# Token mixer: who empties the PSUM banks, when, and how the angles are read

## What is computed

```python
dt = jnp.exp(log_dt)                                   # 128 heads
dt_Lambda = dt * Lambda                                # complex, 64 modes a head
pos = jnp.arange(L)                                    # L = 1024
P = dt_Lambda[..., None] * pos - P_max[..., None]
Wc = Wc * num * _reciprocal(den * Lam, EPS)            # complex weight of a mode, from x
K = jnp.einsum('chn,hnl->chl', Wc, jnp.exp(P)).real    # 64 x 128 x 1024
```

## Time and profile before

| what | value |
|---|---|
| time, median of 3 runs | 6348.16 us (6346.99 to 6351.74) |
| profiled execution: its time, its span | 6355.26 us, 6353.5 us |
| mean granted TensorE clock | 0.973 of full speed |
| busy over the span | PE 92%, DVE 90%, ACT 82%, POOL 90% |

### The profile page before, as it was taken

The page is one execution under the profiler, slowest core; times in us unless marked ns, Lnnn a source line. Parts: engine busy times, 40 slices in busy tenths (PEclk is TensorE's granted clock), DMA queues, the critical chain, the costliest instruction groups (busy, mean ns, idle before and its releaser), DMA issues. The chain is left out here.

```text
span 6353.5 us, 110648 instructions
## 1 busy us (share of the span) xinstructions
PE 5868.1 (92%) x34115; PEld 5413.4 (85%) x34131; DVE 5699.0 (90%) x4609; ACT 5187.5 (82%) x13015; POOL 5718.5 (90%) x3724
## 2 busy tenths in 40 slices
PE   4667899999999999999999999999999999999998
PEld 3433799999999999999999999999899999999997
DVE  7833999999999999999999999999999999999996
ACT  4646788888888888888888888888888888888885
POOL 3501999999999999999999999999999999999995
PEclk8788999999999999999999999999999999999999
DMA  3510122122211222122221222212222122212220
GB/s 80 139 34 32 70 86 76 62 78 86 86 71 64 81 86 81 65 76 81 86 81 60 79 83 86 76 64 77 86 86 70 65 81 86 81 60 79 83 81 33
DMA packets 113795, 478.62 MB, mean 75 GB/s; under 512 B 13345, under 2 KB 50353, under 8 KB 105074
## 3 DMA queue, kind: packets, MB, share of 16 engines
q1 hardware_dynamic: 113266, 471.63, 21.4%
HBM read 328.35 MB, written 143.24 MB: 74 GB/s over the span
## 5 line engine op out<-in xcount | busy, mean ns | idle before, releaser
L1083 POOL TENSOR_TENSOR s_ring<-s_bc,s_u_t 128x820 f32<-128x820 f32 x2048 | 3626.2, 1790 | 3.5 <-DMA s_bc<-rows_bc 3.5
L989 ACT ACTIVATE s_decay<-s_dt_t,a_neg 128x205 f32<-128x205 f32 x8192 | 3047.2, 420 | 428.4 <-DVE s_ring L1154 360.6
L886 PE MATMUL s_y_ps<-s_ring,ident 128*128 128x205 f32 x16384 | 3166.0, 343 | 138.6 <-POOL s_ring L1089 69.0
L886 PEld LDWEIGHTS s_y_ps<-s_ring,ident 128*128 128x128 f32 x16384 | 2888.5, 193 | 227.1 <-POOL s_ring L1089 133.6
L1148 DVE TENSOR_TENSOR_SCAN s_decay<-s_decay,s_ring 128x820 f32<-128x820 f32 x1216 | 2265.4, 1863 | 221.9 <-ACT s_decay L989 219.3
L1089 POOL TENSOR_TENSOR s_ring<-s_ring,s_bc 128x820 f32<-128x820 f32 x832 | 1607.5, 1932 | 52.1 <-DVE s_ring L1148 52.0
L1148 DVE TENSOR_TENSOR_SCAN s_ring<-s_decay,s_ring 128x820 f32<-128x820 f32 x832 | 1543.6, 1855 | 45.2 <-ACT s_decay L989 44.6
L919 PE MATMUL s_xch<-s_x_t,w_low 128*128 128x205 f32 x8192 | 1522.5, 338 | 0.6 <-ACT s_x_t L1029 0.2
L919 PEld LDWEIGHTS s_xch<-s_x_t,w_low 128*128 128x128 f32 x8192 | 1424.1, 190 | 32.8 <-issue 30.5
L1154 DVE TENSOR_TENSOR s_ring<-s_decay,s_bc 128x820 f32<-128x820 f32 x1216 | 1230.1, 1012 | 41.8
L1029 ACT ACTIVATE s_x_t<-s_xch 128x512 f32<-128x512 f32 (+1 forms) x512 | 245.8, 505 | 92.8 <-PE s_xch L910 90.9
(11 more groups left out here) (161 smaller groups left out, 4608.9 us busy)
## 6 DMA issues: line engine op xcount, KB each, us to landing
s_bc<-rows_bc SPq DMA_DIRECT2D x64, 3280.0 KB, 11.2
mixed<-t_res SPq DMA_DIRECT2D x32, 1024.0 KB, 10.3
s_x_in<-mixed SPq DMA_DIRECT2D x64, 512.0 KB
s_h<-mixed SPq DMA_DIRECT2D x64, 512.0 KB
before<-s_h SPq DMA_DIRECT2D x64, 512.0 KB
out<-s_h SPq DMA_DIRECT2D x64, 512.0 KB
s_x_in<-in_txt SPq DMA_DIRECT2D x64, 308.0 KB
s_h<-in_txt SPq DMA_DIRECT2D x64, 308.0 KB
```

What stands on the lines that cost most here:

```text
L886: last = nc.tensor.matmul(y_ps, ident[:, :], ring[:, c % RING, n * LEN:(n + 1) * LEN], start=False, stop=(c % 4 == 3 and n == CN - 1))
L989: last = A.activation(decay[s % 2][:, n * LEN:(n + 1) * LEN], dt_t[:, par, j, :], ACT.Exp, scale=t["a_neg"][:, j, n0 + n:n0 + n + 1])
L1083: nc.gpsimd.tensor_tensor(ring[:, s % RING, :].rearrange("p (n l) -> p n l", n=CN), bc[:, par, n0:n0 + CN, :], u_t[:, j, :].unsqueeze(1).b ...
```

## The change

ScalarE now empties all eight heads, and heads 0 to 3 of group G-1 are emptied between the `Exp` and the `Sin` of step G; heads 4 to 7 follow the `Sin`. VectorE empties none. The angles of a head are computed in two parts: 255 of the 256 positions by eight instructions that read a copy `t_pos_rows` of the positions, laid out as five rows of 51 with a gap of one element behind each row, and the last position of all eight heads by one instruction of 8 elements. The copy is made once.

```diff
-DVE_BANKS = (3,)
...
+        pos_rows = sb("t_pos_rows", [P, 5, 52])
...
-            def evacuate(G, half):
+            def evacuate(G, half, heads):
                 wait(act, out_done[half], out_count(G, half))
-                for h in range(HG):
+                for h in heads:
                     b = h % 4
-                    if b not in DVE_BANKS:
-                        act.wait_ge(full[b], 2 * G + h // 4 + 1)
-                        nc.scalar.activation(res[:, half, h, :, :].rearrange("p b l -> p (b l)"), kb[b][:, :], ACT.Copy).then_inc(empty[b], 1)
+                    act.wait_ge(full[b], 2 * G + h // 4 + 1)
+                    nc.scalar.activation(res[:, half, h, :, :].rearrange("p b l -> p (b l)"), kb[b][:, :], ACT.Copy).then_inc(empty[b], 1)
...
                 last.then_inc(mag_done, 1)
+                if not first:
+                    evacuate(G - 1, 1 - half, range(HG // 2))
                 wait(act, table, 2 * G)
                 act.wait_ge(reduced, G + 1)
                 nc.scalar.activation(osc[:, :], ang[:, :], ACT.Sin, scale=TURN).then_inc(sine_done, 1)
                 if not first:
-                    evacuate(G - 1, 1 - half)
+                    evacuate(G - 1, 1 - half, range(HG // 2, HG))
...
+            L(V.tensor_copy(pos_rows[:, :, 0:51], pos[:, 0:QL - 1].rearrange("p (a b) -> p a b", a=5)))
...
-            def evacuate(G, half):
...
-                        V.tensor_copy(res[:, half, h, :, :].rearrange("p b l -> p (b l)"), kb[b][:, :]).then_inc(empty[b], 1)
...
                 for h in range(HG):
-                    last = V.tensor_scalar(ang[:, h * QL:(h + 1) * QL], pos[:, :], turns[:, bass.ds(G * HG + h, 1)],
-                                           role[:, 1:2], ALU.mult, ALU.add)
-                last.then_inc(turned, 1)
+                    V.tensor_scalar(ang[:, h * QL:(h + 1) * QL - 1].rearrange("p (a b) -> p a b", a=5), pos_rows[:, :, 0:51],
+                                    turns[:, bass.ds(G * HG + h, 1)], role[:, 1:2], ALU.mult, ALU.add)
+                V.tensor_scalar(ang[:, QL - 1::QL], turns[:, bass.ds(G * HG, HG)], pos[:, QL - 1:QL], role[:, 1:2],
+                                ALU.mult, ALU.add).then_inc(turned, 1)
```

More of the change, by code:

```diff
@@ L294, in step @@
                 if not first:
-                    evacuate(G - 1, 1 - half)
-            loop(act, step, evacuate)
+                    evacuate(G - 1, 1 - half, range(HG // 2, HG))
+            loop(act, step, lambda G, half: evacuate(G, half, range(HG)))
         @block.gpsimd
@@ L420, in step @@
                             last.then_inc(crossed, 1)
-                if not first:
-                    evacuate(G - 1, 1 - half)
-            loop(dve, step, evacuate)
+            loop(dve, step)
         @block.tensor
```

## The result

The changed kernel takes 6330.87 us (median of 7 runs, 6323.80 to 6332.09), the kernel before 6349.17 (7 runs, 6346.99 to 6355.06): ratio 0.9967, 95% interval 0.9958 to 0.9976, so about 18 us or 0.33% faster. The forecast was 6318 in a range of 6299 to 6342, with 6310 to 6325 for its likeliest case. The gain is real and smaller than forecast, and the time lies outside the likeliest case's own range.

The account below looks back on a forecast made before the run. The prediction took a ring of waits to bound the mixer's step: 15 x (17.49 - 15.5) = 29.9, less 1.6, plus 2.0, gives 30 us; 6325 profiled, 6318 as median, range 6299 to 6342.

Parts of the forecast that it names:

- likeliest case: Mixer steps set by Ring P and Ring E by turns, 14.8 or 16 us; 6310 to 6325 us, chance 0.49.
- eight angles of 255: VectorE's angles in the mixer: unpaired, no wait for GpSimd, 0.455 us each, eight in 3.64 us.
- The instruction of 8: VectorE's last positions in the mixer: taken as paired, so waiting for GpSimd; under 0.29 us itself.
- Ring P: Mixer step through GpSimd's products p1 to p4, then VectorE's rounding and subtraction, then the sine: 14.8 us.
- Ring E: Mixer step through p2, heads 0 to 3, their evacuations, table load, sine: 13.5 us at full clock, 16.0 partly at half.
- first rival: TensorE stays cold longer, half-clock stretch every mixer step: all steps 16.3 us, 18 us gained, 6330 us; chance 0.2.
- Ends: Outside the mixer's steps: 1.6 us lost before the first sine, 2.0 us gained behind the last evacuation.
- The signs of error: Trace signs against the forecast: angles wait, ScalarE waits for `t_kb` before every sine, or next stage later than 320 us.
- The rule on two SBUF operands: Skill's rule that such VectorE instructions wait for GpSimd's port; set aside, letting the subtraction run beside p4; 2.3 us at stake.
- second rival: VectorE's rounding slips in behind GpSimd's p3: Ring P 12.5 us, steps mean 14.4, 46 us gained, 6302 us; chance 0.13.
- What bounds the mixer now: In the kernel before: a ring of waits through sine, slow heads, head 7's copy, angles and subtraction, 17.49 us a step.
- From trace to median: Whole kernel: the median of runs taken 7.1 us below the profiled execution, so 6325 became 6318 us.

Follow-up runs that it names:

- e8: The kernel before with twenty unused identity matmuls added on TensorE behind head 7 in each step: 6350.89 us, ratio 1.0002.
- e7: The changed kernel with twenty unused identity matmuls per step, and eight angles of 256 reading positions from PSUM, no 8-element instruction: 6308.53 us, ratio 0.9934.
- e2: The kernel before with the change's new angles alone, evacuations as before: 6346.95 us, ratio 0.9994.
- the probe: The changed kernel with a separate block ahead of the mixer, VectorE instructions beside back-to-back GpSimd products; only its rows are read, no kernel time.
- e10: The changed kernel with twenty unused matmuls per step, positions and the rounding's constant read from PSUM, two evacuations ahead of the sine: 6300.78 us, ratio 0.9923.
- e6: The changed kernel with two evacuations ahead of the sine and six behind it: 6313.10 us, ratio 0.9941.
- e11: The changed kernel with positions and the rounding's constant read from PSUM, two evacuations ahead of the sine, no added matmuls: 6295.89 us, ratio 0.9918.
- e3: The changed kernel with twenty unused identity matmuls added on TensorE behind head 7 in each step: 6312.62 us, ratio 0.9944.

## Why the prediction was partly right

- **The angles** (*eight angles of 255*): right. 3.65 us for eight, 3.64 forecast, beside GpSimd without a wait.
- **The instruction of 8**: right, it takes a turn at the port, 0.28 undisturbed and up to 2.41.
- **Ring P**: right, 14.8 forecast, 14.75 where the clock is kept up or two evacuations stand ahead. One premise was off: GpSimd was taken as never delayed. In the step shown after, p1 to p4 take 10.25 us (168.14 to 178.39) and not 9.3, since p4 waits for the rounding.
- **Ring E**: its price was right (13.5 at full clock, 16.0 with a stretch at half clock; 15.2 to 16.5 measured). **The term that was mis-sized is how often that stretch comes**: "some steps are 14.8 and some 16; I take 15.4". It came in every step, so no step was 14.8, the twelve steps average 15.92, and with the first three (16.1, as forecast) 15.95 in place of 15.5. That is 15 x 0.45 = 6.8 us, nearly all of the 7.3 by which the trace's gain of 22.75 falls short of 30. This is the first rival, which had 0.2: a fall in every step. Its time of 6330 is the measured one partly by luck. It took 16.3 a step, where the prediction's own price of ring E, 16.0, was what came; in the trace it would have gained 18 and the change gained 22.75. The argument against it, that TensorE's share of work rises, didn't count. The pause in front of p2, 5.20 us here, did: the earlier trace rows showed 4.3 at 1.00 ahead of a fall, and the sum should have taken a pause that long as a fall each time. Why the clock fell each time is not shown beyond that: in e8 it fell behind a pause of 1.96 us as well.
- **Ends**: 1.85 lost ahead of the first sine for 1.6; 1.5 won at the tail for 2.0.
- **The signs of error**: two of the three came. ScalarE waits for `t_kb` ahead of the sine in all 15 steps (the first rival's sign), and the next stage starts later than 320, at 321.92.
- **The rule on two SBUF operands**: the row chosen against it shows a product with one operand in PSUM, and says nothing of two in SBUF. It cost nothing in the sum, because where ring P decides, the subtraction comes behind p4 anyhow; in the second rival it would have, as e7 shows.
- **What bounds the mixer now**: the slow heads were named as part of the ring of before. By e8 a step of that kernel was set by p4's end, through the paired angles. With those gone and head 7 still waited for (e2) it was little shorter (17.07 where most were 17.31). That is why the change needed both halves.
- From trace to median: the forecast took 7.1 off; the two profiled executions are 25.6 us apart (22.75 in the mixer, 2.9 behind it, where nothing was changed) and the medians 18.3. Single executions of either kernel lie within 8.3 us of one another, so a few us between a trace and a median say nothing.

What stays open: whether five rows escape the port by their odd count or by their unequal shapes. Seven elements on both sides waited (2.26 us in the probe), which speaks for the second. Five rows written as five rows did not wait (0.54), but those outputs lie without a gap; whether the engine got them as five rows or as one run no run shows, and an output with gaps was not tried.

## What to carry to other kernels

When two rings have nearly the same length, price each at both clock levels, and take the slow level for every step in which TensorE pauses as long as it did ahead of a fall in the trace. Before adding work to TensorE to keep the clock up, look at where it ends: in e10 it made head 0 2.1 us late. Put ahead of a releasing instruction on an in-order queue only as much as buffers need: two evacuations did all that four did, and even none did better than four; with two, TensorE's half clock cost nothing in e6 and at most 0.2 us a step in e11. Where VectorE and GpSimd meet at the port, look at where the operands lie: an operand in PSUM, even with a slower form, can shorten the step.

## What the hardware showed

- In the probe VectorE and GpSimd take the port by turns, one instruction each: beside products of 2.33 us, one of 1.01 lasts 3.03, and GpSimd's 3.10; neither is favoured.
- Eight elements can cost 2.4 us (0.28 undisturbed), since they too wait for the end of GpSimd's instruction.
- A VectorE instruction with one operand in SBUF and one in PSUM kept 2.29 us for 2048 elements beside GpSimd, where two SBUF operands took 4.31.
- The clock fell in or right behind a pause of 5.17 to 6.19 us in 15 of 15 steps, and each fall lengthened the next step's first heads: head 0 took 2.05 to 2.08 us, 1.13 at full clock in e3.
